# Two buffers for the attention input x and a different mixed order of two instruction streams, in an eleven-layer sequence kernel on one core

## What is computed

```python
x = norm(x + attn0(x))      # x += causal attention, 16 heads of 8, keys from a latent of 32;
                            # x += local attention, window 32 (each on rmsnorm(x))
x = norm(x + moe(x))        # 8 experts 128->512->128 with gelu, all computed, top-2 gates
x = norm(x + linear(x))     # elu+1 linear attention, 64 wide, as a scan over tokens
x = norm(x + local(x))      # 2 layers: token shift, qkv (8 heads of 64), l2norm, rotary,
                            # attention in windows of 64, wo, layernorm, 128->341*2 gated gelu, 128
```

## Time and profile before

| what | before |
|---|---|
| median of 3 runs | 2710.54 us (2708.66 to 2717.31) |
| profiled execution, its own time | 2714.04 us |
| span of the profiled execution | 2711.9 us |
| PE (TensorE matmul) busy | 2055.0 us, 76% |
| VectorE, ScalarE, GpSimd busy | 1307.6, 1275.7, 595.2 us |
| mean granted TensorE clock, of full speed | 0.83 |

### The profile page before, as it was taken

The page is one execution under the profiler, slowest core; times in us unless marked ns, Lnnn a source line. Parts: engine busy times, 40 slices in busy tenths (PEclk is TensorE's granted clock), DMA queues, the critical chain, the costliest instruction groups (busy, mean ns, idle before and its releaser), DMA issues.

```text
span 2711.9 us, 38853 instructions
## 1 busy us (share of the span) xinstructions
PE 2055.0 (76%) x14843; PEld 1280.8 (47%) x14843; DVE 1307.6 (48%) x2660; ACT 1275.7 (47%) x2638; POOL 595.2 (22%) x505
## 2 busy tenths in 40 slices
PE   2855975688679997478877998658877899767786
PEld 1123754333446674233454666433344567445454
DVE  3133224643645535554355444564355453557574
ACT  2642321367435761156633665137743566225453
POOL 1420000354111200244301120025411120024231
PEclk8776985689879997678877999758987899778888
DMA  3000100000000100000000110000000010000000
GB/s 101 1 1 1 32 16 8 12 13 25 1 9 24 28 20 4 16 13 13 21 5 4 36 28 9 7 21 9 11 19 9 16 36 21 4 16 21 13 17 13
DMA packets 32058, 45.50 MB, mean 17 GB/s; under 512 B 7823, under 2 KB 18947, under 8 KB 31747
## 3 DMA queue, kind: packets, MB, share of 16 engines
q1 hardware_dynamic: 31875, 43.01, 5.9%
HBM read 24.12 MB, written 2.10 MB: 10 GB/s over the span
## 4 chain that ended last, share of the span: by engine, by line
PE 51%; DVE 25%; ACT 9%; issue 8%; POOL 5%; SPq 1%; DMA 0%; DVEq 0%; ACTq 0%; POOLq 0%
PE PD L859 8%; PE PH L899 7%; PE PH L682 4%; PE PB L1048 4%; PE PB L1068 3%; POOL front_arena L1901 3%; ACT front_arena L1179 2%; ACT back_arena L1311 2%; PE PB L984 2%; PE PB L1005 2%; PE PD L726 2%; DVE back_arena L1783 2%; PE PB L1104 2%; DVE back_arena L1782 2%; POOL fy L1943 1%
## 5 line engine op out<-in xcount | busy, mean ns | idle before, releaser
L1179 ACT ACTIVATE front_arena<-PD 128x1024 f32<-128x1024 f32 (+3 forms) x384 | 296.3, 818 | 159.4 <-PE PD L726 158.1
L1938 POOL TENSOR_TENSOR back_arena<-back_arena 128x512 f32<-128x512 f32 x128 | 171.8, 1344 | 904.3 <-DVE back_arena L1783 903.9
L899 PEld LDWEIGHTS PH<-W,front_arena 128*128 128x128 f32 x2048 | 250.8, 192 | 70.1 <-issue 36.7
L899 PE MATMUL PH<-W,front_arena 128*128 128x128 f32 x2048 | 267.8, 278 | 19.9 <-DVE R L1629 19.6
L1048 PE MATMUL PB<-wqkv,hT 128*128 128x512 f32 x384 | 242.9, 725 | 45.5 <-DVE back_arena L1783 41.6
L1268 ACT ACTIVATE front_arena<-PD,b 128x512 f32<-128x512 f32 x256 | 162.0, 684 | 235.9 <-PE PD L859 235.4
L1901 POOL TENSOR_TENSOR front_arena<-front_arena,tri 128x256 f32<-128x256 f32 x256 | 198.0, 788 | 327.7 <-ACT front_arena L1179 327.4
L859 PE MATMUL PD<-xT,W 128*128 128x512 f32 x512 | 254.8, 622 | 1.2 <-ACT xT L1162 1.2
L1790 DVE TENSOR_REDUCE fnm<-PB 128x4 f32<-128x512 f32 x128 | 88.5, 691 | 338.4 <-PE PB L1068 337.4
L682 PE MATMUL PH<-front_arena 128*32 128x512 f32 (+3 forms) x1536 | 192.4, 578 | 61.4 <-POOL front_arena L1901 42.5
L1943 POOL TENSOR_TENSOR fy<-fm,minus_half 128x16 f32<-128x16 f32 x64 | 187.9, 2936 | 105.0 <-DVE fm L1806 103.6
(11 more groups left out here) (241 smaller groups left out, 3393.3 us busy)
## 6 DMA issues: line engine op xcount, KB each, us to landing
W<-in_W SPq DMA_DIRECT2D x32, 512.0 KB, 3.4
back_arena<-back_arena SPq DMA_DIRECT2D x128, 128.0 KB, 2.3
X<-in_L_attn_hidden SPq DMA_DIRECT2D x64, 32.0 KB, 1.9
out_y<-Nb SPq DMA_DIRECT2D x64, 32.0 KB, 1.6
wqkv<-in_L_ffn_wqkv SPq DMA_DIRECT2D x1, 1536.0 KB
back_arena<-in_c_xpos SPq DMA_DIRECT2D x1, 1024.0 KB
back_arena<-in_L_ffn_w SPq DMA_DIRECT2D x1, 682.0 KB
wo<-in_L_ffn_wo SPq DMA_DIRECT2D x1, 512.0 KB
```

Source lines behind the costliest of these rows:

```text
L899: ins = pe.matmul(p[:, 128 * t:128 * t + 128], hv[:, c, 128 * t:128 * t + 128], W12[e % WRING][:, HF + 128 * c:HF + 128 * c + 128], start= ...
L1179: act.activation(pb[:, :, 0:n], p[:, :, 0:n], ACT.Exp, scale=INV_SQRT_HD).then_inc(freed(b, "S", half, g, kc, jp), 1)
L1938: pool.tensor_tensor(T1[k % 2][:, hs, :], T1[k % 2][:, hs, :], T2[:, hs, :], ALU.add).then_inc(sg("rot"), 1)
```

## The change

It does two things.

**x has two buffers**, `XX[0]` and `XX[1]`, used by sequences b even and odd, with a semaphore each (`x_in0`, `x_in1`). The load for sequence b+1 is queued at `x1` of sequence b, ahead of the later expert weights, and waits for the back of sequence b-1 to have taken its x. `back_arena` shrinks by 2 KB (it had that to spare) to make room.

**The table ORDER is made in another way.** Each step now has four numbers: TensorE time, time to the end of the step alone, ScalarE time and VectorE time. `order()` walks both lists with a small model of three engines. At each turn it takes the stream whose next step could start sooner; when both could within 0.05, the one with the longer rest ahead of it. A back starts only after its front, a front b starts only after the back of b-2 has taken its x. So front and back of a pair no longer start and end together.

```diff
+    def add(label, pe=0.0, alone=0.0, act=0.0, dve=0.0):
+        out.append((label, (pe, max(pe, alone), act, dve)))
...
-        add(5, "nrm", a)
+        add(("nrm", a), 0, 8, 0, 7)
...
-                add(1.9, "h", i, k)
+                add(("h", i, k), 1.9, 1.9, 1.4)
...
 def order():
-    out = [("F", i) for _, i in whole(FRONT, 0)]
-    for b in range(B):
-        back = [(x, 1, "B", i) for x, i in whole(BACK, b)]
-        front = [(x, 0, "F", i) for x, i in whole(FRONT, b + 1)] if b + 1 < B else []
-        out += [(who, i) for _, _, who, i in sorted(back + front)]
+    while at["F"] < B * len(FRONT) or at["B"] < B * len(BACK):
+        options = []
+        for who, labels in streams.items():
...
+            start = ready[who]
+            if who == "B" and i == 0:
+                if b not in front_ends:
+                    continue
+                start = max(start, front_ends[b])
+            if who == "F" and i == 0 and b >= 2:
+                if b - 2 not in taken:
+                    continue
+                start = max(start, taken[b - 2])
+            (p, _, a, v) = labels[i][1]
+            start = max(start, pe if p else 0, act - 3, dve - 3)
+            behind = left[who][i] + (B - 1 - b) * left[who][0] + (left["B"][0] if who == "F" else 0)
+            options.append((start, -behind, who))
+        soonest = min(o[0] for o in options)
+        start, _, who = min((o for o in options if o[0] <= soonest + 0.05), key=lambda o: o[1])
...
-        X = sb("X", [128, NT, 128])
+        XX = [sb(f"X{i}", [128, NT, 128]) for i in range(2)]
...
-                        if b:
-                            sp.wait_ge(sg("x_taken"), 2 * b)
-                            read(sp, b - 1, "fxF", 0, 1)
-                        src = batch(x_in, b)
+                        if b + 1 < B:
+                            yield front_at(b, "x1", 0)
+                            if b:
+                                sp.wait_ge(sg("x_taken"), 2 * b)
+                                read(sp, b - 1, "fxF", 0, 1)
+                            load_x(b + 1)
+                        for e in range(WRING, E):
+                            yield front_at(b, "h", 2 * (e - WRING) + 3, 0)
+                            read(sp, b, "eo", 2 * (e - WRING) + 1)
+                            load_expert(e)
...
-                        dve.wait_ge(sg("x_in"), 256 * (b + 1))
+                        dve.wait_ge(sg(f"x_in{b % 2}"), 256 * (b // 2 + 1))
```

More of the change, by code:

```diff
@@ L125, in front_labels @@
                 for n, u in enumerate(attention_units(half)):
-                    add(1.1, "S", half, *u)
+                    add(("S", half, *u), 0.65, 1.05, 0.8, 0.1)
                     if half:
@@ L226, in back_labels @@
             if l and i == 0:
[L227 removed]
+                add(("nF", 0, 1), 0.9, 2, 0.6, 0.7)
             if l and i == 1:
```

230 lines of the change are left out of this document (121 added, 109 removed).

## The result

The kernel after takes **2647.09 us** (median of 4 runs, 2645.18 to 2649.28), against 2709.6 us of the kernel before on the same chip (2705.01 to 2717.31). The ratio is 0.9767, 95% interval 0.9743 to 0.9791: 2.3% faster. The forecast was 2610, so the sign and the range held, and some 63 us came where 100 were expected.

A forecast was written before the change was run, and what follows sets the result against it. No engine is full; 40% of back steps stand beside the experts, where they cannot be absorbed. Back-step prices in the pairs fall from 655 to 555 us, 100 less, giving 2610 us, range 2500 to 2690.

The forecast's parts named there:

- What bounds the kernel: 84 of 211 back steps per pair stand beside the experts, where each costs all of its own TensorE time.
- 1. Experts: Fronts 1 and 2 run experts alone, weight loads hidden; 87 steps beside front 3 at 1.10 cost 96 us, before 278.
- 2. Causal: Causal stages of the pairs: 299 back steps where there were 183, at 0.85 us each, 254 us.
- 3. Middle: Middle stages of the pairs: 113 back steps where there were 87, at 0.64 us each, 72 us.
- 4. Setup 0: Setup 0 of the pairs: 13 steps at 1.12 (15 us) and 42 at 0.64 (27 us), together 42 us.
- 5. End: End stages of the pairs: 67 back steps at 0.91 us each, 61 us.
- 6. Tail: After front 3, the last 12 steps of back 2 run with nothing beside them: 30 us, a new serial piece.
- 7. x: Start of fronts: early load removes the 30.8 us wait for x; later starts of backs and the loads cost nothing.
- A: Gaps fill: back steps beside stages other than the experts mostly cost the middle's 0.64 us; near 2530 us, chance 0.28.
- B: Only the wait for x goes; back steps cost 1.04 us on average wherever they stand; near 2680 us, chance 0.10.
- C: Slower: back work in GpSimd's strict queue delays the causal stage's masks, up to 127 us, 2737 us; chance 0.07.

The follow-up runs named there:

- late_in_pairs: Kernel after, with the back's one-time tables built in front 0 and value products one score unit later in sequences 1 to 3 only: 2608.91 us.
- early_tables: Kernel after, with the back's one-time tables built on VectorE in front 0 instead of at the first back's start: 2632.24 us.
- two_x_old_order: Kernel before, with the second x buffer and early load but the old front labels and table ORDER: 2689.19 us, ratio 0.9916.
- warm_front0: late_in_pairs plus 48 f16 products, whose results nobody reads, in front 0's causal stage: 2609.88 us.
- old_pattern: Kernel after, part of fronts 1 and 2's causal back steps moved beside their experts, streams there alternating as in the kernel before: 2665.7 us.
- late_and_early: Kernel after, with the back's tables built in front 0 and value products later in all sequences: 2634.89 us, ratio 0.9705.
- no_tail: Kernel after, with one back step per front step beside the experts of sequence 3, 99 instead of 87: 2649.82 us.

## Why the prediction was right, and where its sizes were off

**What bounds the kernel**: right in that a step beside the experts costs all of its TensorE time, not shown in that it costs less in the causal stage. Where the shift was undone inside the new order it cost 40, 35 and 19 us (the last with the old pattern). But from before to after a step saved beside the experts gave 1.16 us and one added in the causal stage took 1.29. What the order won is, by the table, rather in the end (19 us less with 25 steps more), setup 0 (8) and the stretches between fronts (9 beyond what the buffer gave).

**1. Experts**: right. Fronts 1 and 2 run them in 118.4 and 118.1 us, TensorE 99% busy, so the weights' loads stayed hidden. The 87 steps beside front 3 cost 86 us, 0.99 each instead of 1.10.

**2. Causal: the step that failed.** It took 0.85 us a step from the row of 61 steps and multiplied it by 299. It came to 0.99, 41 us more (all three pairs before had 145.2 / 183 = 0.79; pair 2 was the dearest). The 0.85 was not a price per step. In pair 2 before, busy x clock is 142.88 x 0.90 = 128.6 us, that of front 0 alone 92.37 x 0.77 = 71.1, so 61 steps add 57.5, 0.94 each; after, 181.49 x 0.89 = 161.5, so 95 steps add 90.4, 0.95 each. The work per step hardly changed (over all three pairs 0.93 and 0.97). What made 61 of them look cheap is that the front's own 71.1 run at 0.90 in 79.0 us instead of 92.4: 13.4 us given back, once per pair, however many steps there are. Dividing it by 61 and multiplying by 299 counts 13.4 x (299/61 - 3) = 25 us that do not exist. The other 16 are idle time and work per step, about half each. In pair 2 of the table, the 12.2 us by which 93.0 exceeds 95 x 0.85 = 80.8 are 7.5 from this, 1.9 from idle time and 2.8 from the clock (0.89 for 0.90) and the work per step; a hundredth of the clock is 2 us here, so the parts are no finer than that. Behind it stood the reading that a back step after each unit would fill the 25.6 us of gaps. The rows spoke against it: 61 steps had left the 24.3 us of front 0 unfilled. They grew, to 28.2. Groups on PE of pair 2's causal stage:

```profile
L716 PE MATMUL PH<-front_arena 128*32 128x512 f32 (+3 forms) x384 | 45.7, 552 | 20.1 <-POOL front_arena L1936 13.2 <-DVE front_arena L1582 6.9
L760 PE MATMUL PD<-front_arena 32*128 32x512 f16 (+3 forms) x192 | 33.7, 356 | 5.4 <-DVEq L1597 3.9 <-ACT front_arena L1213 1.2 <-ACT front_arena L1201 0.3
```

The value products of L716 wait for the masks of their own units, which stand behind the back's work on GpSimd, or for VectorE, and the back's ready products stand behind them in TensorE's queue: a table of more back steps cannot fill a gap that opens at the head of the queue. Moving the value products later won 29.5 us over the causal stages of the pairs (late_in_pairs), a third of it idle time and the rest clock.

**3. Middle**: right, 73.8 for 72.

**4. Setup 0**: 63.5 for 42. Two errors. In pair 1, 13 steps cost 22.7 us, not 15, as the first back's tables lie there, which the row of pair 2 did not have: 6.4 us left with early_tables. And the 42 steps of fronts 2 and 3 cost 9.4 + 31.4 = 40.8 us, 0.97 each: the price of the middle, 0.64, did not carry over to its twin.

**5. End**: 41.6 for 61, 0.62 a step. The 0.91 came from a stage with 14 steps; here 67 hide better under VectorE's chains. It almost pays for term 4, and that is luck: the terms of setup 0, causal, middle and between fronts were 69 us too low together, those of experts, end and tail 34 too high, and only so the sum is no more than 36 off.

**6. Tail**: 25.8 for 30, as foreseen.

**7. x**: the wait of L1481 (now L1516) has no row for x any more, and two_x_old_order shows its 30 us in the windows. What replaces it is 5.1 us between fronts. Backs 1 and 2 start inside the causal stage with no gap ahead of them; the first waits 19.1 us, where it waited 12.9 in the kernel before. The loads, costed at nothing, cost nothing that the rows show.

**The rivals.** A fell: TensorE is busy 76%, not over 80 (nor the 79 of the forecast), and the clock 0.845, not 0.86; the gaps did not fill. (Its mean clock of 0.78 is weighted by time; by PE's busy time the rows give 0.80.) Its thought about the clock was sound as a lever: late_in_pairs gained its time with 0.98 in pair 1. B fell as a whole: two_x_old_order stands at 2689 and after at 2647, but its kernel of truth is term 2, where each further step costs all of its own TensorE time. C fell in size: it put up to 127 us on GpSimd's queue, and the wait of L716 for masks went from 12.3 to 13.2 us in pair 2. But its mechanism is in the trace: 8.6 of those 13.2 us are masks behind the back's work on GpSimd, and that is why masks of 8 columns took only 4.4 of them away. The masks themselves went from 808 to 826 ns:

```profile
L1936 POOL TENSOR_TENSOR front_arena<-front_arena,tri 128x256 f32<-128x256 f32 x64 | 52.1, 826 | 66.9 <-ACT front_arena L1213 66.7
```

For the loss to VectorE the prediction had named the Trainium skill (GPSIMD Engine Reference, section Specifications), where GpSimd's SBUF interfaces are shared with VectorE, and had worked out 50 ns a mask from the rows. It was 18 ns, 3.5 us in all and not 9, so leaving it out of the sum was closer. That VectorE is what slows the masks is not shown by any run here.

## What to carry to other kernels

A price per added step, read from a stage with one mix, holds only for that mix. Split it first: work as busy time times granted clock, which adds up per step, then what a better clock gives the other stream, which comes once, then the gaps, and ask of each gap whether it opens at the head of an in-order queue, where no added work can fill it, and what stands ahead of its releaser in that engine's own queue. A second buffer is worth more than the wait it removes if it widens what the order may choose from, and an order that uses that freedom needs it: each alone was worth 22 us or was a loss, both together 63. And a measure that helps where two streams run can cost as much where one runs alone, so make it depend on the stage.

## What the chip showed that I had not expected

- The clock of one stage reacts strongly to where small waits fall. With 60 to 62 steps in the causal stage of pair 1 the granted clock was 0.79, 0.83, 0.86 and 0.90, with 99 steps 0.92, 0.96 and 0.98, and each hundredth is some 2 us (128 us of work at 0.80, or 168 at 0.95). More back steps did not order it, nor did TensorE's busy share alone (0.84 to 0.89).
- The same 632 products took 92.4 us at 0.77 in front 0 and 117.4 us at 0.57 with 46 waits of half a microsecond for ScalarE between them, where there had been 19. None of these waits is longer than 0.9 us. The Trainium skill (TensorE: Matmul & The Clock Gate, section What's actually happening) has the lower rate as the default that activity lifts; that agrees. That 48 products for nobody lift it from 0.79 to 0.84 and still save nothing is what warm_front0 adds.
- What stays open: why the pattern of the kernel before gives 0.90 there and 0.83 in old_pattern, and why the middle and end of pair 1 take 10 us less in some runs (early_tables, late_and_early, no_tail) than in others (after, late_in_pairs, warm_front0). Gains of that size in one stage are not to be read as the effect of an edit.
